# Turning the next group's weights: TensorE transposes replaced by a DMA transpose of 16-bit halves, with GpSimd splitting and joining

## What is computed

```python
proj = jnp.einsum('bld,pd->blp', hidden_states, in_proj_w)      # in_proj_w: 10304 x 512
gate, hbc, dt = proj[..., :I], proj[..., I:I + CONV_DIM], proj[..., -H:]
xBC = silu(causal_conv(hbc, conv_weight) + conv_bias)           # x, B, C
# per head: state = state * dA_t + dtx_t * B_t ;  y_t = state . C_t
y = ys + x * D
yn = group_rms_norm(y) * norm_weight * silu(gate)
out = jnp.einsum('bli,di->bld', yn, out_proj_w)
```

## Time and profile before

| | |
|---|---|
| median of 3 runs | 3419.07 us (3419.03 to 3420.64) |
| profiled execution, span | 3417.9 us |
| TensorE matmuls, busy | 3395.8 us (99%) |
| TensorE weight loads, busy | 2869.8 us (84%) |
| VectorE, busy | 3025.9 us (89%) |
| ScalarE, busy | 1406.9 us (41%) |
| GpSimd, busy | 446.0 us (13%) |
| granted TensorE clock, mean | 0.999 of 2.4 GHz |
| DMA | 466.23 MB, 136 GB/s over the span |

### The profile page before, as it was taken

One profiled execution on the slowest core, in us unless ns is written; L12 is line 12 of the kernel. 1 busy time (PEld: TensorE's weight loads), 2 busy tenths in 40 slices (PEclk: granted clock), 3 DMA queues, 4 the chain that ended last, 5 costly groups with the idle time before them and its releaser, 6 DMA issues. The chain is left out here.

```text
span 3417.9 us, 58378 instructions
## 1 busy us (share of the span) xinstructions
PE 3395.8 (99%) x19738; PEld 2869.8 (84%) x19738; DVE 3025.9 (89%) x4815; ACT 1406.9 (41%) x2179; POOL 446.0 (13%) x328
## 2 busy tenths in 40 slices
PE   8999999999999999999999999999999999999999
PEld 6788888888888888888888888888888888888888
DVE  6899999999999999999999999999999999998443
ACT  5555553444434444344443444434444334433111
POOL 1111111011110111101111011110111100111333
PEclk9999999999999999999999999999999999999999
DMA  7433263234432353325433262335423352225331
GB/s 270 172 117 123 105 226 132 107 135 161 159 130 109 135 191 128 131 108 191 136 128 132 107 221 106 127 132 181 148 106 127 131 181 94 76 95 154 93 92 59
DMA packets 207789, 466.23 MB, mean 136 GB/s; under 512 B 35134, under 2 KB 80606, under 8 KB 198284
## 3 DMA queue, kind: packets, MB, share of 16 engines
q1 hardware_dynamic: 206364, 464.72, 38.8%
q0 software_dynamic: 368, 0.85, 0.1%
q10 hardware_dynamic: 1024, 0.27, 0.0%
HBM read 313.68 MB, written 152.09 MB: 136 GB/s over the span
## 5 line engine op out<-in xcount | busy, mean ns | idle before, releaser
L1119 PE MATMUL p_cv<-ht,wt 128*128 128x512 f32 x5376 | 1274.5, 392 | 0.8 <-DVE xc L1343 0.8
L1119 PEld LDWEIGHTS p_cv<-ht,wt 128*128 128x128 f32 x5376 | 1004.0, 188 | 224.3 <-issue 11.0
L1211 PE MATMUL bank<-wot,gy 128*128 128x512 f32 x3072 | 728.3, 392 | 0.0
L1211 PEld LDWEIGHTS bank<-wot,gy 128*128 128x128 f32 x3072 | 571.9, 188 | 121.0
L1252 ACT ACTIVATE xc<-p_cv,cvb,cvw 128x512 f32<-128x512 f32 x256 | 200.0, 782 | 898.6 <-PE p_cv L1119 898.4
L1343 DVE SCALAR_TENSOR_TENSOR xc<-p_cv,cvw,xc 128x496 f32<-128x496 f32 (+2 forms) x768 | 545.0, 717 | 22.1 <-ACT xc L1252 0.2
L1119 PE MATMUL bank<-ht,wt 128*128 128x512 f32 x2304 | 554.6, 390 | 0.0
L1119 PEld LDWEIGHTS bank<-ht,wt 128*128 128x128 f32 x2304 | 431.9, 188 | 89.3
L1071 POOL TENSOR_TENSOR r<-rv,neg_half 128x4 f32<-128x4 f32 x64 | 89.5, 1398 | 2345.0 <-DVE rv L1423 2345.0
L1065 POOL TENSOR_TENSOR segr<-adts,mask_le 128x1024 fp32r<-128x1024 f32 x128 | 243.0, 1920 | 424.0 <-DVE adts L1326 424.0
L1361 DVE TENSOR_TENSOR m<-cbm,y 128x1024 f32<-128x1024 f32 x256 | 295.9, 1218 | 0.0
(11 more groups left out here) (191 smaller groups left out, 3418.1 us busy)
## 6 DMA issues: line engine op xcount, KB each, us to landing
ht<-h_d SPq DMA_DIRECT2D x63, 2048.0 KB, 7.9
acc_d<-acc SPq DMA_DIRECT2D x64, 1024.0 KB, 4.3
wt_d<-wnext SPq DMA_DIRECT2D x112, 512.0 KB, 3.4
acc<-acc_d SPq DMA_DIRECT2D x56, 1024.0 KB, 7.1
wt<-wt_d SPq DMA_DIRECT2D x70, 512.0 KB, 8.4
stage<-in_L_attn_in_proj_w SPq DMA_DIRECT2D x84, 256.0 KB, 2.8
wot<-wt_d SPq DMA_DIRECT2D x28, 512.0 KB, 6.4
xb<-in_x SPq DMA_DIRECT2D x8, 1024.0 KB, 8.3
```

Of the source, the lines that this page charges most:

```text
L1119: ins = pe.matmul(pb[:, :], wt[:, n, l, k, :], ht[:, rr, k, :], start=(q == 0 and k == 0), stop=(q == 2 and k == KC - 1))
L1211: ins = pe.matmul(bank[OUT[t]][:, :], gy[:, c, l, t * P:(t + 1) * P], wot[:, rr, c, :], start=(c == 0 and q == 0), stop=(c == CT - 1 and q ...
```

## The change

The eight transposes on TensorE and their PSUM banks go. In their place, for each of the two chunks u: GpSimd copies the 1024 16-bit halves of a partition's 512 words from `stage[u]` into two planes, all low halves and all high halves (`halves`, 128 x 2 x 512, uint16); SyncE issues a DMA transpose of the eight 128 x 128 blocks into `turned`; GpSimd copies them back, interleaved, into `stage[u]`, which then holds the turned fp32 words. ScalarE makes the high part from `stage[u]` in SBUF. GpSimd in place of VectorE subtracts it for the low part. `halves` and `turned` lie where `wnext` lies, so a split waits until the last `wnext` is stored (`s_nst`).

In GpSimd's program `prepare_next(it)` stands between `scan_products(it)` and `root(it)`: two splits, two joins, two subtractions. In SyncE's queue the two transposes stand behind the load of `acc`, and in a turn iteration inside the loop of weight loads, ahead of the chunk n = 6. ScalarE's copies stay where they were, between `gate(2)` and `high(0)`, and wait for the joins. TensorE no longer waits for `s_raw` or `s_nlo`.

```diff
+    halves = [nc.alloc_sbuf_tensor_at(f"halves{u}", [P, 2, DM], U16, offset=sh.wnext_at + 8 * DM * u) for u in range(2)]
+    turned = [nc.alloc_sbuf_tensor_at(f"turned_halves{u}", [P, 2, DM], U16, offset=sh.wnext_at + 8 * DM * u + 4 * DM) for u in range(2)]
...
+        def turn_next(it):
+
+            for u in range(2):
+                sp.wait_ge(s_nsplit, 2 * it + u + 1)
+                sp.sem_inc(s_ngo, 1)
+                sp.dma_start_transpose(turned[u][:, :, :].rearrange("p a (k c) -> p (a k) c", c=P),
+                                       halves[u][:, :, :].rearrange("p a n -> p (a n)")).then_inc(s_nturn[u], 16)
...
+            if not last and not turn:
+                turn_next(it)
             if turn:
                 for n in range(NPJ - 1):
+                    if n == NCV:
+                        turn_next(it)
                     sp.wait_ge(s_proj, NPJ * it + n + 1)
...
+        def words(u):
+
+            return stage[u][:, :].bitcast(U16).rearrange("p (n a) -> p n a", a=2)
+
+        def prepare_next(it):
+
+            for u in range(2):
+                pool.wait_ge(s_raw[u], 16 * it + 16)
+                pool.wait_ge(s_nst, 32 * it + 32)
+                pool.sem_inc(s_nready, 1)
+                pool.tensor_copy(halves[u][:, :, :].rearrange("p a n -> p n a"), words(u)).then_inc(s_nsplit, 1)
+            for u in range(2):
+                pool.wait_ge(s_nturn[u], 16 * it + 16)
+                pool.sem_inc(s_nready, 1)
+                pool.tensor_copy(words(u), turned[u][:, :, :].rearrange("p a n -> p n a")).then_inc(s_njoin, 1)
+            for u in range(2):
+                pool.wait_ge(s_nhi, 2 * it + u + 1)
+                pool.tensor_tensor(wnext[:, u, 1, :], stage[u][:, :], wnext[:, u, 0, :].bitcast(F32),
+                                   ALU.subtract).then_inc(s_nlo, 1)
...
+        with pool.Fori(1 + R, NBLK * (G - 1)) as it:
+            scan_products(it)
+            prepare_next(it)
+            root(it)
+        with pool.Fori(NBLK * (G - 1), NIT - 1) as it:
             scan_products(it)
             root(it)
...
-            for u in range(2 if prepare else 0):
-                pe.wait_ge(s_raw[u], 16 * it + 16)
-                pe.wait_ge(s_z, CT * it + CT + 1 + u)
-                for k in range(KC):
-                    ins = pe.transpose(bank[NEXT[u]][:, k * P:(k + 1) * P], stage[u][:, k * P:(k + 1) * P], sh.ident[:, :])
-                ins.then_inc(s_nps, 1)
...
-            if prepare:
-                pe.wait_ge(s_nlo, 2 * it + 1)
...
-            if prepare:
-                pe.wait_ge(s_nlo, 2 * it + 2)
...
-                act.wait_ge(s_nps, 2 * it + u + 1)
-                act.wait_ge(s_nst, 32 * it + 32)
-                act.activation(wnext[:, u, 0, :], bank[NEXT[u]][:, :], ACT.Copy).then_inc(s_nhi, 1)
+                act.wait_ge(s_njoin, 2 * it + u + 1)
+                act.activation(wnext[:, u, 0, :], stage[u][:, :], ACT.Copy).then_inc(s_nhi, 1)
...
-            for u in range(2 if prepare else 0):
-                dve.wait_ge(s_nhi, 2 * it + u + 1)
-                dve.tensor_tensor(wnext[:, u, 1, :], bank[NEXT[u]][:, :], wnext[:, u, 0, :].bitcast(F32),
-                                  ALU.subtract).then_inc(s_nlo, 1)
```

More of the change, by code:

```diff
@@ L22 @@
 U8 = mybir.dt.uint8
+U16 = mybir.dt.uint16
 ALU = mybir.AluOpType
@@ L896, in attend_part @@
     bank = sh.bank
-    XT, SEG, CB, YB, OUT, SSQ, NEXT = (3, 4, 5, 7), (5, 7), 6, (6, 7, 4, 5), (2, 3, 4, 5), 6, (0, 1)
+    XT, SEG, CB, YB, OUT, SSQ = (3, 4, 5, 7), (5, 7), 6, (6, 7, 4, 5), (2, 3, 4, 5), 6
     s_raw = [sem(f"s2_raw{u}") for u in range(2)]
-    s_nps = sem("s2_nps")
+    s_nsplit = sem("s2_next_split")
+    s_nturn = [sem(f"s2_next_turned{u}") for u in range(2)]
+    s_njoin = sem("s2_next_joined")
+    s_nready = sem("s2_next_operands_ready")
+    s_ngo = sem("s2_next_turn_may_start")
     s_nhi = sem("s2_nhi")
@@ L1083, in gpsimd_part @@
         pool.wait_ge(sh.s_mask, 4)
+        prepare_next(0)
         root(0)
@@ L1099, in gpsimd_part @@
             pool.wait_ge(sh.s_cbq, spread)
+            prepare_next(1 + s)
             root(1 + s)
-        with pool.Fori(1 + R, NIT - 1) as it:
+        with pool.Fori(1 + R, NBLK * (G - 1)) as it:
[3 more added lines that the diff above has]
+        with pool.Fori(NBLK * (G - 1), NIT - 1) as it:
             scan_products(it)
```

## The result

The changed kernel takes 3722.7 us (median of 4 runs, 3718.61 to 3725.23) against 3419.31 us (3419.03 to 3420.64) for the kernel before, a ratio of 1.0884 with a 95% interval of 1.0869 to 1.0899. It is 303 us slower, 5.4 us for each of the 56 prepared iterations. The prediction said 3409.5, with a range up to 3500.

A forecast was written before the change was run, and what follows sets the result against it. TensorE, never idle, bounds the kernel; 32 iterations keep 0.15 us and 24 keep 0.20, 9.6 us in all, other parts nothing: 3419.07 - 9.6 = 3409.5 us. Own range 3406.7 to 3412.9; for 8 in 10, 3402 to 3500.

The forecast's parts named there:

- The bound and the cover: TensorE never idles; its transposes cover the `dtx` products, so only 0.15 to 0.20 us per prepared iteration is kept, 9.6 in all.
- the cushion: VectorE's 1.33 us of idle before `dtx`, which can absorb delays before TensorE's scan has to wait.
- Rival D: At TensorE's scan: if `scan(0)` didn't wait for all of `dtx`, the whole 49 us come out, 3370; chance 0.04.
- GpSimd's split: On GpSimd: each split takes 1.9 us, bounded by rows of 1.30 and 1.92; splits end at 1024.8 and 1026.7.
- Rival A: GpSimd's joins hold VectorE's products m, delaying `dtx`: 33 us (3443) if one join blocks, 141 us (3550) if both; chance 0.20.
- The joins in time: DMA transposes take 5 us and GpSimd's joins end by 1034, 10 us before 1044.6, so ScalarE's wait costs nothing.
- Rival B: DMA transposes land late in every iteration, from 9 us each; TensorE waits for `low`: 3528 at 10 us, 4199 at 16; chance 0.14.
- Rival C: Late landings behind a full queue in the seven turn iterations alone: 14 to 35 us, 3424 to 3445; chance 0.09.
- VectorE's subtractions worth nothing: Two subtractions fewer on VectorE, 1.29 us behind `dtx`, gain nothing because TensorE doesn't wait for what they bring forward.
- GpSimd's subtractions: Two on GpSimd, 1.3 us each, follow ScalarE's copies and end near 1041.6, as VectorE's do; store and load keep their places.

The follow-up runs named there:

- transposes away: Kernel before without TensorE's eight transposes, nothing in their place; ScalarE and VectorE read the raw chunk in `stage`, weights of groups 1 to 7 unturned: 3411.6 us.
- short split: Changed kernel with GpSimd's split copy reading with a stride and writing one plane after the other: 3411.7 us, ratio 0.9973.
- `pair` was out of the way: Changed kernel, long split, with the four `pair` and the comparison moved from between the taps to behind `times_dt`: 3516.5 us, ratio 1.0277.
- projection 8 as the cover: Projection 8 moved behind `turn_x` in prepared iterations: on the changed kernel with stride-reading split 3376.6 us; on the kernel before without transposes 3403.4 us.

## Why the prediction was wrong, by its steps

**The bound and the cover: right.** The transposes were the cover of `times_dt`. Without them, and with nothing held beyond the cushion, the time is 3411.6 (transposes away) and 3411.7 us (short split), against a forecast of 3409.5. Against the kernel before, run beside them at 3420.86, that is a gain of 9.2 us, where 9.6 were forecast. The period is 47.30 in both, against "47.3 in place of 47.45". The gain per iteration of 0.15 to 0.20 us stands. Rival D, the whole 49 us, was rightly put low.

**GpSimd's split: the step that failed first.** "I take 1.9, since 1024 are also written, with a stride." It takes 5170 ns, 2.7 times the upper bound of 1.92. That bound came from 32-bit operations that write in order, of which none writes 16-bit elements to two places in turn. I named the stride and gave it no price of its own: 1.9 is the row of 1024 elements. The same copy with the stride on its reading side takes 1131 ns, below the lower bound of 1.30. The join, which reads in turn from the two planes and writes in order, takes 1464 (1345 with the short split), inside the range. An access pattern that no row shows is not bounded by rows of other patterns; the upper end of the range should have been left open there, and what a long split meets should have been asked.

**What the split meets: the second failure.** Rival A looked for VectorE instructions "which read two SBUF tensors" and so found only m, at the joins. It passed over `pair`, which has one large input, although it lies right where the splits run, and so put that wait at nothing. Measured it is 6.25 us per iteration. A row could have hinted at it. A product of two 128 x 512 inputs takes 684 ns, and `pair` on the same size 539: it runs faster than the others, and of VectorE's instructions beside the splits it is the fast one that was stopped. My argument against a hold of whole instructions, a predicated copy inside `root`, was about another kind of instruction beside a GpSimd one of four elements, and said nothing about `pair` or m beside a long one. (No run has a predicated copy beside a split, so whether it would be held stays open.) As for the size: A had 0.6 to 2.5 us per iteration, measured are 5.5. At its own place A was right in kind, 0.39 us on m in the changed kernel and 2.71 once `pair` was out of the way, but it wasn't the term that decides.

**The joins in time: right.** The two transposes land after 3.0 us each (median; 5.0 with the short splits, when both are issued at once), where 5 was taken. The last join ends at 1134.0, ScalarE's copies begin at 1138.78, and it waited for a join 19.3 us in 9 times in all, in the turn iterations and right behind them. Rival B (9 us or more for each) is out. The Trainium skill's 1309 ns for a block of 128 x 128 (VectorE: DVE Perf Modes, "The three transpose paths") does not add up over eight blocks here: an estimate of 10.5 us from that figure, 3.0 measured. Rival C is out as well where nothing else is late: with the short split the turn iterations and those behind them have the common period but for two, 0.8 and 1.1 us longer. With the long split the iterations behind the turns cost the 8 us named above.

**VectorE's subtractions worth nothing: right, for this order.** With them moved to GpSimd 3411.7, without 3411.6. With projection 8 as the cover it is no longer so: 3376.6 against 3403.4, 27 us. "Worth nothing" was true of the present bound and hid what the move could bring with one more edit.

**GpSimd's subtractions:** 1.3 us taken, 1274 ns with the short split; 1669 in the changed kernel, where VectorE's m often runs beside the first of the two and GpSimd is the one that is held (2.20 us at 1139.48, beside an m that began at 1139.34; 1.27 for the second, beside `dtx`).

## What to carry to other kernels

Before work goes to GpSimd, list VectorE's instructions in the same stretch by kind, not only by length. Here a one-input one that is shorter than its size suggests (539 against 684 ns) and one with two inputs in SBUF (m) stopped until GpSimd's instruction ended, and ones with an input in PSUM did not. Short GpSimd instructions (1.1 us here) hide in a cushion that one of 5.2 us overruns. Write a reordering copy so that its writes are contiguous and its reads carry the stride. And when an edit frees an engine whose next wait follows at once, look for other work to put in front of that wait: here the edit itself gave 0.3%, and one projection moved behind `turn_x` another 1.0%.

## What the runs showed of the hardware

- A GpSimd copy of 1024 16-bit elements per partition takes 5.17 us when it writes to two planes in turn and 1.08 to 1.13 us when it reads them in turn; a memset in the alternating order takes 4.9 us, one of 4096 fp32 elements in order 3.54.
- While such an instruction runs, an int32 tensor_scalar of 128 x 512 on VectorE (0.54 us alone) takes up to 5.1 us, and beside two memsets in a row 9.79 us. A GpSimd instruction that only writes, the memset, is enough to hold it. Taps with one operand in PSUM keep their 0.70 to 0.73 us beside the splits, and `dtx`, also with one, its 0.68 beside GpSimd's subtractions. m, with two inputs in SBUF, takes 2.18 us beside a join of 1.4 to 1.9 and 1.22 alone.
- A DMA transpose of 128 x 1024 16-bit elements, SBUF to SBUF, lands 3.0 us after its issue, little longer than a plain load of the same bytes (2.7 to 2.8).
- TensorE's mean granted clock was 0.978 of 2.4 GHz in the changed kernel and 0.999 before, with waits in every iteration where there had been none. No run separates what that adds to the 303 us; the comparison of iterations with the same hold gives 0.4 us for each one that it touches.
